# First attention of a perceiver block: the row norms of the distances made by TensorE products in PSUM instead of a VectorE addition

## The reference, cut to what matters

```
q = einsum('tbm,mhd->tbhd', x, q_weight)
q_sq = einsum('tbhd,tbhd->tbh', q, q)
squared_dist = q_sq[:, None] + q_sq[None, :] - 2 * einsum('tbhd,sbhd->tsbh', q, q)
attn_weights = softmax(-squared_dist * inv_sqrt_d, axis=1)
PXA = einsum('tsbh,sbhm->tbhm', attn_weights, XA)
```

## Time and profile before

| what | us |
|---|---|
| median of three timed executions | 594.95 (593.56 to 595.21) |
| the profiled execution, its own time | 591.21 |
| its span, first to last instruction | 589.4 |
| TensorE busy in it | 574.4 |
| VectorE, ScalarE, GpSimd busy | 351.5, 201.7, 221.2 |

### The profile page before, as it was taken

One profiled execution on the slowest core, in us unless ns is written; L12 is line 12 of the kernel. 1 busy time (PEld: TensorE's weight loads), 2 busy tenths in 40 slices (PEclk: granted clock), 3 DMA queues, 4 the chain that ended last, 5 costly groups with the idle time before them and its releaser, 6 DMA issues.

```text
span 589.4 us, 11467 instructions
## 1 busy us (share of the span) xinstructions
PE 574.4 (97%) x4860; PEld 494.4 (84%) x4864; DVE 351.5 (60%) x410; ACT 201.7 (34%) x286; POOL 221.2 (38%) x182
## 2 busy tenths in 40 slices
PE   6999999999999999999999999999999999999997
PEld 6989888898989889797778988978888887888886
DVE  4887771826546182652597257567777446875741
ACT  3544343505234351513602451423341122434320
POOL 2599963565626265560325000203333543000000
PEclk9999999999999999999999999999999999999999
DMA  8763423141213324005102502206822421798601
GB/s 305 275 237 131 152 79 146 71 151 71 76 76 101 122 71 151 1 1 176 35 2 74 152 3 72 66 8 148 219 72 74 140 71 72 173 259 203 151 1 71
DMA packets 25284, 65.76 MB, mean 112 GB/s; under 512 B 2424, under 2 KB 2424, under 8 KB 22304
## 3 DMA queue, kind: packets, MB, share of 16 engines
q1 hardware_dynamic: 25248, 65.23, 35.7%
HBM read 64.05 MB, written 1.18 MB: 111 GB/s over the span
## 4 chain that ended last, share of the span: by engine, by line
PE 79%; DVE 6%; POOL 5%; issue 2%; ACT 1%; POOLq 0%; DVEq 0%
PE ps L317 16%; PE ps L319 15%; PE ps L318 15%; PE ps L823 8%; POOL psum_tmp L455 4%; PE ps L846 3%; PE ps L850 3%; PE ps L838 2%; PE ps L833 2%; PE ps L832 2%; PE ps L902 2%; PE ps L837 2%; DVE stats L1309 1%; PE ps L864 1%; PE ps L1113 1%
## 5 line engine op out<-in xcount | busy, mean ns | idle before, releaser
L455 POOL TENSOR_TENSOR psum_tmp<-psum_tmp,raw 128x512 f32<-128x512 f32 (+1 forms) x88 | 139.9, 1589 | 34.3 <-DVE lo L1336 25.8
L823 PE MATMUL ps<-hi 128*128 128x256 f32 (+3 forms) x416 | 129.7, 313 | 4.8 <-ACT hi L537 4.8
L823 PEld LDWEIGHTS ps<-hi 128*128 128x128 f32 (+1 forms) x416 | 78.9, 190 | 5.3 <-ACT hi L537 4.8
L1336 DVE TENSOR_TENSOR lo<-raw,hi 128x2048 fp32r<-128x2048 f32 (+1 forms) x29 | 61.7, 2159 | 24.4 <-ACT hi L529 24.4
L317 PE MATMUL ps<-hi,gh 128*128 128x512 f32 x192 | 75.7, 394 | 0.0
L319 PE MATMUL ps<-hi,gl 128*128 128x512 f32 x192 | 74.8, 390 | 0.0
L318 PE MATMUL ps<-lo,gh 128*128 128x512 f32 x192 | 74.8, 390 | 0.0
L510 POOL TENSOR_TENSOR sx<-sx,raw 128x512 f32<-128x512 f32 x32 | 41.0, 1290 | 82.3 <-DVE raw L1664 82.3
L710 ACT ACTIVATE hi<-raw 128x2048 fp32r<-128x2048 f32 x14 | 26.8, 1914 | 93.0 <-PE ps L319 83.6
L317 PE MATMUL ps<-wvh,gh 128*128 128x512 f32 x128 | 50.9, 398 | 0.0
L319 PE MATMUL ps<-wvh,gl 128*128 128x512 f32 x128 | 50.0, 391 | 0.0
(11 more groups left out here) (218 smaller groups left out, 1197.6 us busy)
## 6 DMA issues: line engine op xcount, KB each, us to landing
raw<-in_ctx SPq DMA_DIRECT2D x23, 1024.0 KB, 4.8
raw<-in_ve SPq DMA_DIRECT2D x8, 1024.0 KB, 5.3
raw<-in_oe SPq DMA_DIRECT2D x8, 1024.0 KB, 5.4
wk<-gm_rows SPq DMA_DIRECT2D x8, 512.0 KB, 9.1
g<-gm_rows SPq DMA_DIRECT2D x8, 512.0 KB, 9.7
raw<-in_ctx SPq DMA_DIRECT2D x8, 130.0 KB
xres<-in_x SPq DMA_DIRECT2D x1, 1024.0 KB, 9.8
mb<-in_WqT SPq DMA_DIRECT2D x1, 1024.0 KB, 13.5
```

Of the source, the lines that this page charges most:

```text
L455: pool.tensor_tensor(psum_tmp[0:k, :], (raw[:, 0, :] if t == 1 else psum_tmp[0:k, :]), raw[0:k, t, :], ALU.add).then_inc(ctx_sum, 1)
L823: pe.matmul(dst, hi[0:kk, t, cols], x, start=start and opens, stop=stop and closes, skip_group_check=True)
L1336: dve.tensor_tensor(lo[0:k, r, :], raw[0:k, r, :], hi[0:k, r, :].bitcast(F32), ALU.subtract).then_inc(ctx_lo, 1)
```

## The change

The product of the queries no longer closes the accumulation in a near bank. Behind each group of four such products (one for each head) stand four new ones that have the squares `xn` as weights and the constant -0.5 (`neghalf`, 64 columns) as moving operand, so the row's half norm is added in PSUM. `half_norms`, the ScalarE copy into `sqb`, the tensor `sqb` and VectorE's `near_add` are gone. ScalarE takes the exponential from PSUM, in two instructions for each pair of chunks, each of two banks (1024 columns). The second `distances` waits for ScalarE instead of VectorE. `near_norm(0)` is cut in two halves, two reciprocals and two multiplications. The numbers in the other waits follow from that.

```diff
         headmask = sb("headmask", [P, P])
         samepos = sb("samepos", [P, 8])
         apart = sb("apart", [P, 8], BF16)
-        sqb = sb("sqb", [P, KC, NG, 4])
         rowrec = sb("rowrec", [P, KC, 4 * NG])
         causal = sb("causal", [P, 4 * P], BF16)
         neghalf = sb("neghalf", [P, S])
@@ -167,8 +166,8 @@
         att_mm, y_done, xb_done, z_done, x1_done, ob_done = (
             sem(s) for s in ("att_mm", "y_done", "xb_done", "z_done", "x1_done", "ob_done"))
         qq_done, vv_mm, vv_done, samepos_done = (sem(s) for s in ("qq_done", "vv_mm", "vv_done", "samepos_done"))
-        d_mm, d_add, d_exp, sqb_mm, sqb_done, d_rec, nv_mm, nv_done, vv_ones = (
-            sem(s) for s in ("d_mm", "d_add", "d_exp", "sqb_mm", "sqb_done", "d_rec", "nv_mm", "nv_done", "vv_ones"))
+        d_mm, d_exp, d_rec, nv_mm, nv_done, vv_ones = (
+            sem(s) for s in ("d_mm", "d_exp", "d_rec", "nv_mm", "nv_done", "vv_ones"))
         lg_mm, mx_done, nm_done, e_done, eT_mm, eT_done = (
             sem(s) for s in ("lg_mm", "mx_done", "nm_done", "e_done", "eT_mm", "eT_done"))
         pT_mm, pT_hi, pT_lo, op_mm, x2_done = (sem(s) for s in ("pT_mm", "pT_hi", "pT_lo", "op_mm", "x2_done"))
@@ -648,13 +647,12 @@
                 act.activation(grouped(qT[:, k, :]), natural(q1_bank(k)[:, :]), ACT.Copy).then_inc(q_done, 1)
                 act.activation(grouped(xn[:, k, :]), natural(q1_bank(k)[:, :]), ACT.Square).then_inc(qq_done, 1)
 
-            act.wait_ge(sqb_mm, 1)
-            act.activation(sqb[:, :, :, :].rearrange("p c g j -> p (c g j)"), bank[3][:, 0:KC * NG * 4], ACT.Copy,
-                           scale=-0.5).then_inc(sqb_done, 1)
-
-            def nearness(c):
-                act.wait_ge(d_add, 2 * c + 2)
-                act.activation(near_heads_of(c), near_heads_of(c), ACT.Exp, scale=2.0 * INV1).then_inc(d_exp, 1)
+            def nearness(p, m):
+
+                act.wait_ge(d_mm, p + 1)
+                src = ps[:, near_bank(2 * m):near_bank(2 * m) + 2, :].rearrange("p j (c n) -> p j c n", c=2)
+                dst = kv[:, 4 * p:4 * p + 4, :].rearrange("p k n -> p (k n)").rearrange("p (c j n) -> p j c n", c=2, j=4)
+                act.activation(dst[:, 2 * m:2 * m + 2, :, :], src, ACT.Exp, scale=2.0 * INV1).then_inc(d_exp, 1)
 
             def values_out(g):
                 act.wait_ge(vv_mm, g + 1)
@@ -665,12 +663,12 @@
                 act.wait_ge(pT_mm, c + 1)
                 act.activation(natural(wvh[:, c, :]), grouped(turn_bank(c)[:, :]), ACT.Copy).then_inc(pT_hi, 1)
 
-            nearness(0)
-            nearness(1)
+            nearness(0, 0)
+            nearness(0, 1)
             values_out(0)
             values_out(1)
-            nearness(2)
-            nearness(3)
+            nearness(1, 0)
+            nearness(1, 1)
             near_high(0)
             near_high(1)
             w_high(W_Q2, 0, 2)
@@ -1055,7 +1053,7 @@
                 if p == 0:
                     pe.wait_ge(samepos_done, 2)
                 else:
-                    pe.wait_ge(d_add, 4)
+                    pe.wait_ge(d_exp, 2)
                 for j in range(4):
                     pe.matmul(bank[near_bank(j)][:, :], identb[:, :], apart[:, :].unsqueeze(1).broadcast_to([P, S, 8]),
                               start=True, stop=False, skip_group_check=True)
@@ -1074,24 +1072,18 @@
                             for j in range(4):
                                 row = slice(D1 * j, D1 * j + D1)
                                 dst = ps[S * cg:S * cg + S, near_bank(j), c * 2 * P + g * S:c * 2 * P + g * S + S]
-                                mm = pe.matmul(dst, qT[row, 2 * p + c, tok], qT[row, 2 * p + c, tok], start=False, stop=True,
-                                               skip_group_check=True)
+                                pe.matmul(dst, qT[row, 2 * p + c, tok], qT[row, 2 * p + c, tok], start=False, stop=False,
+                                          skip_group_check=True)
+                            for j in range(4):
+                                row = slice(D1 * j, D1 * j + D1)
+                                dst = ps[S * cg:S * cg + S, near_bank(j), c * 2 * P + g * S:c * 2 * P + g * S + S]
+                                mm = pe.matmul(dst, xn[row, 2 * p + c, tok], neghalf[row, :], start=False, stop=True, skip_group_check=True)
                 mm.then_inc(d_mm, 1)
 
-            def half_norms():
-
-                for c in range(KC):
-                    pe.wait_ge(qq_done, c + 1)
-                    for g in range(NG):
-                        mm = pe.matmul(bank[3][:, (c * NG + g) * 4:(c * NG + g) * 4 + 4], xn[:, c, g * P:(g + 1) * P],
-                                       headmask[:, :].rearrange("p (h d) -> p h d", d=D1)[:, :, 0], start=True, stop=True)
-                mm.then_inc(sqb_mm, 1)
-
             def head_values():
 
+                pe.wait_ge(qq_done, KC)
                 for g in range(NG):
-                    if g == NG - 1:
-                        pe.wait_ge(sqb_done, 1)
                     for c in range(KC):
                         pe.wait_ge(q_done, KC + c + 1)
                         mm = pe.matmul(vv_bank(g)[:, c * P:(c + 1) * P], qT[:, c, g * P:(g + 1) * P], cb[:, c, :], start=True, stop=True)
@@ -1099,12 +1091,10 @@
 
             def near_values(c):
 
-                pe.wait_ge(d_exp, c + 1)
+                pe.wait_ge(d_exp, c // 2 * 2 + 2)
                 if c == 0:
                     pe.wait_ge(vv_ones, 1)
                     pe.wait_ge(vv_done, NG)
-                if c == 2:
-                    pe.wait_ge(d_add, 8)
                 for g in range(NG):
                     for j in range(4):
                         for cg in range(2):
@@ -1117,14 +1107,13 @@
 
             def turn_values(c):
 
-                pe.wait_ge(nv_done, c + 1)
+                pe.wait_ge(nv_done, c + 2)
                 for g in range(NG):
                     tok = slice(g * P, (g + 1) * P)
                     mm = pe.transpose(turn_bank(c)[:, tok], mb[:, c, tok], ident[:, :])
                 mm.then_inc(pT_mm, 1)
 
             distances(0)
-            half_norms()
             head_values()
             distances(1)
             near_values(0)
@@ -1532,17 +1521,6 @@
             dve.memset(vv[:, :, :, D1:D1 + 1], 1.0).then_inc(vv_ones, 1)
             w_low(W_OUT, 1)
 
-            def near_add(c):
-
-                dve.wait_ge(d_mm, c // 2 + 1)
-                for m in range(2):
-                    if c == 0 and m == 0:
-                        dve.wait_ge(sqb_done, 1)
-                    row = sqb[:, c, :, 2 * m:2 * m + 2].rearrange("p g j -> p j g").unsqueeze(3).broadcast_to([P, 2, NG, S])
-                    dve.tensor_tensor(near_heads_of(c)[:, 4 * P * m:4 * P * m + 4 * P].rearrange("p (j g n) -> p j g n", j=2, n=S),
-                                      ps[:, near_bank(2 * m):near_bank(2 * m) + 2, pair(c % 2)].rearrange("p j (g n) -> p j g n", n=S),
-                                      row, ALU.add).then_inc(d_add, 1)
-
             def values_out(g):
 
                 dve.wait_ge(vv_mm, g + 1)
@@ -1552,24 +1530,24 @@
             def near_norm(c):
 
                 dve.wait_ge(nv_mm, c + 1)
-                dve.reciprocal(rowrec[:, c, :].rearrange("p (k h) -> p k h", k=2), num_heads(c)[:, :, :, D1]).then_inc(d_rec, 1)
-                dve.wait_ge(d_rec, c + 1)
-                per_head = rowrec[:, c, :].rearrange("p (k h) -> p k h", k=2).unsqueeze(3).broadcast_to([P, 2, 8, D1])
-                dve.tensor_tensor(mb[:, c, :].rearrange("p (k h d) -> p k h d", k=2, d=D1), num_heads(c)[:, :, :, 0:D1], per_head,
-                                  ALU.mult).then_inc(nv_done, 1)
+                ks = (slice(0, 1), slice(1, 2)) if c == 0 else (slice(0, 2),)
+                sums_of = [rowrec[:, c, :].rearrange("p (k h) -> p k h", k=2)[:, k, :] for k in ks]
+                for k, sums in zip(ks, sums_of):
+                    dve.reciprocal(sums, num_heads(c)[:, k, :, D1]).then_inc(d_rec, 1)
+                dve.wait_ge(d_rec, c + 2)
+                for k, sums in zip(ks, sums_of):
+                    per_head = sums.unsqueeze(3).broadcast_to([P, k.stop - k.start, 8, D1])
+                    dve.tensor_tensor(mb[:, c, :].rearrange("p (k h d) -> p k h d", k=2, d=D1)[:, k, :, :], num_heads(c)[:, k, :, 0:D1],
+                                      per_head, ALU.mult).then_inc(nv_done, 1)
 
             def near_low(c):
                 dve.wait_ge(pT_hi, c + 1)
                 dve.tensor_tensor(natural(wvl[:, c, :]), grouped(turn_bank(c)[:, :]), natural(wvh[:, c, :].bitcast(F32)),
                                   ALU.subtract).then_inc(pT_lo, 1)
 
-            near_add(0)
-            near_add(1)
             values_out(2)
             values_out(3)
-            near_add(2)
             near_norm(0)
-            near_add(3)
             near_norm(1)
             near_low(0)
             near_low(1)
```

## The result

The changed kernel took 599.61 us (median of 9 executions, 594.87 to 603.94), the kernel before 594.18 us (9 executions, 590.51 to 595.76). The ratio is 1.0089, with a 95% interval of 1.0061 to 1.0117: slower by 0.9%. One of the nine executions after (603.94) is over 1.5% above the fastest of its kernel; such slow ones are left out of every ratio here and kept in the medians. The forecast was 592.9, in a range of 591.4 to 595.4. The profiled execution of the changed kernel took 601.69 us for a span of 600.0, against 591.21 and 589.4 before.

A forecast was written before the change was run, and what follows sets the result against it. The prediction took TensorE, busy for 97% of the span, as the bound. Its terms, -3.87 - 1.46 + 3.50 - 0.25 = -2.08 us, put on the median of 594.95, gave 592.9 us, with 591.4 to 595.4 for 8 in 10.

The forecast's parts named there:

- Term 1: half_norms goes; its 32 matmul records hold TensorE alone, so -3.87 us.
- Term 2: head_values runs at full clock once half_norms is gone, 3.55 us where it took 5.01: -1.46 us.
- rival A: The clock's fall before or in head_values gives nothing back: -0.6 us, so 594.3 us; chance 0.27.
- Term 3: New row products in both calls of distances, at 13.7 ns each: +3.50 us, bounds +2.4 and +7.7.
- rival C: Eight products in a row on four tiles run at L1113's pace, +7.7 us: slower, 597.1 us; chance 0.1.
- Terms 4 to 7: near_add goes, -0.25 us; exponentials from PSUM, near_norm(0) in halves, and the dropped ScalarE copy and swapped waits: 0.

The follow-up runs named there:

- wide_norms2: The kernel before with 128 moving columns, side by side in memory, in place of 4 in each product of half_norms; median 590.5 us.
- no_row: The changed kernel without its 128 row products, the exponent scaled by 0.001; median 588.9 us, 587.1 at clock 1.00.
- order4: The changed kernel with the same instructions reordered so that column halves alternate after four products, as in the kernel before; median 603.0 us.
- interleave: The changed kernel with the four groups of head_values spread inside and between the calls of distances; median 597.6 us, 592.6 at clock 1.00.
- pad128: The changed kernel with 128 empty TensorE instructions at the start, which never reached the program, so the same program again; median 603.1 us.
- wide_values: The changed kernel with 64 moving columns in place of 33 in each product of near_values; median 596.2 us, 594.8 at clock 1.00.

## Why the prediction was wrong

- **Term 1, half_norms: right.** It went, and head_values starts right behind the first distances.
- **Term 2, the clock: right in its place, wrong as a sum.** head_values ran at 1.00, -1.24 us in the profile for the -1.46 forecast, and wide_norms2 confirms the cause. It was also sized from an execution with a mean clock of 0.997, while half of all have 0.994: from 0.994 to full clock the kernel before has 2.6 us to gain (594.0 to 591.4). But the prediction took the clock to be up afterwards, from the row of L1113 at 1.00. The mean clock fell from 0.994 to 0.990, 2 us at 0.4 (kernel before) to 0.5 (changed kernel) for 0.001. That row came from an execution without a hole in front; with holes and 33 columns together the clock fell, with 64 columns only briefly. The prediction named 0.50 anywhere near as what would prove it wrong, and gave rival A only the loss of the gain, not a larger fall than before.
- **Term 3, the row products: the step that failed.** Their own time was +3.48 us for the +3.50 forecast. What failed is the reading of 12.4 ns for a record as a pace that can be kept up. It held for 128 loads and 128 matmuls, exactly one block of 256 instructions, 1.6 us; with 256 and 256 in a row the blocks don't come as fast. That cost 4.19 us of holes, which no term contained. The prediction bounded the price from above by L1113, +7.7, and the measured one is 7.67 in the profile and 7.8 at full clock (changed kernel against no_row): that the bound comes near is luck. It stood for rival C, with 0.1, and for another mechanism: not the order and not the PSUM cells (order4: 0.2 us a call) but the fetch.
- **Terms 4 to 7: right.** The exponentials took 0.97 us each, just under the 1.0 to 1.15 forecast, and nobody waited for them; near_norm(0) needs 0.28 for both reciprocals and 0.76 for both products; in interleave, whose clock stayed up, TensorE's wait before turn_values(1) is 0.49, as forecast. In no_row the edits other than the products give -4.3 us at full clock.
- **The sum** at full clock: -4.3 + 3.5 + 4.2 = +3.4, measured +3.5 (591.4 to 594.9, the latter a single execution). That they meet within 0.1 is partly luck, since the holes of the same program were 4.9 us in pad128. With 2 us from the clock that is the +5.4 of the medians.

The rule of the Trainium skill cited for term 3 ("TensorE: Matmul & The Clock Gate", Part 3), by which a load of weights overlaps running matmuls only where the row group differs, neither caught nor caused the miss. The 3.2 that the prediction worked out by it lies near the 3.48 of run time, and it has no holes either. The Trainium skill ("TensorE: Matmul & The Clock Gate", Part 1) says that the gate's look at activity runs freely, and the spread of the mean clock from 0.986 to 1.00 over the executions of the kernel before agrees.

## What to carry to other kernels

A short burst of small products shows a pace that TensorE can't keep: before products are added, count the instructions (an f32 product is four) against the blocks of 256, and spread them between long products. A group whose products stream few columns can lower the clock of the group behind it; widening the moving operand as far as the load of weights hides it cost nothing measurable here and took 0.65% off this kernel. And where executions differ, sort them by granted clock first; the time at full clock and the mean clock answer two separate questions.

## What the runs showed of the hardware

- TensorE's instructions come in blocks of 256; the queue that brings them moves packets of 16 KB. With 12 to 13 ns for a load and its matmul a block lasts 1.6 us, and holes of 0.4 to 2.1 us appear at block ends, each over 1.2 to 1.6 us after a packet has landed. Not every block end has one.
- A hole of 0.7 to 1.9 us and near_values' products of 33 columns together go with a long fall of the clock (20.5 us at half clock in no_row, 13.7 in the changed kernel); with 64 columns the fall behind the same holes was 3.4 us (wide_values), and with 33 columns and no hole the mean clock was 1.000 (wide_norms2).
- A moving operand of 128 f32 columns of which neighbours lie 128 bytes apart takes 7.21 us for 32 matmuls, the same columns side by side 3.66.
- At full clock a load of 128 columns of f32 weights sets the pace at 0.11 us (28 steps in 3.12 us, 32 in 3.66) whether 4 or 128 columns are streamed behind it, but with 4 of them the clock fell (mean 0.994 over 70 executions), with 128 hardly (1.000 over 10).
